# Feed-forward stage of a cross-attention block: inner Hadamard rotation in blocks of 128 on TensorE, one more butterfly level on VectorE and GpSimd, and half the down projection ahead of the transposes

## What is computed

```python
def fwht(x):            # Hadamard transform along the last axis, n a power of 2
    h = 1
    while h < n:
        x = x.reshape(-1, n // (2 * h), 2, h)
        a, b = (x[:, :, 0, :], x[:, :, 1, :])
        x = jnp.stack([a + b, a - b], axis=2).reshape(-1, n)
        h *= 2
    return (x * (1.0 / np.sqrt(n))).reshape(orig_shape)

def h_bitlinear(x, w):
    xq = act_quant(fwht(x))     # per token: scale to 127 by the largest magnitude, round
    wq = weight_quant(w)        # -1, 0 or 1 times one scale
    return jnp.einsum('bsh,oh->bso', xq, wq)
gate = h_bitlinear(hidden_states, w_gate)       # 512 -> 2048
up = h_bitlinear(hidden_states, w_up)
return h_bitlinear(jax.nn.silu(gate) * up, w_down)   # fwht over 2048, then 2048 -> 512
...
x = x + _L0_xattn_ref(_layernorm(x, axis=-1), ctx_1024, ...)
x = x + _L0_ffn_ref(_layernorm(x, axis=-1), ...)
```

## Time and profile before

| | us |
|---|---|
| median of 3 runs | 1434.11 |
| lowest, highest | 1431.78, 1435.32 |
| the profiled execution, its own time | 1431.52 |
| its span | 1429.4 |
| TensorE busy (share of the span) | 1396.0 (98%) |
| VectorE, ScalarE | 943.6, 943.4 (66% each) |
| GpSimd | 514.5 (36%) |

### The profile page before, as it was taken

How to read it: one execution, slowest core, us unless ns; L and a number is a source line. 1 busy time by engine, 2 the same in 40 slices (tenths; PEclk the granted TensorE clock), 3 DMA queues, 4 the chain that set the end, 5 groups by cost and what they waited for, 6 DMA issues and landing times. The chain is left out here.

```text
span 1429.4 us, 25937 instructions
## 1 busy us (share of the span) xinstructions
PE 1396.0 (98%) x8471; PEld 1198.2 (84%) x8471; DVE 943.6 (66%) x2401; ACT 943.4 (66%) x2068; POOL 514.5 (36%) x320
## 2 busy tenths in 40 slices
PE   8999989999999999999999999998999999999998
PEld 7999868999999999999999999997766677767775
DVE  5312047677777777777777777765466777767775
ACT  4556668888888888888888888887424333433432
POOL 0033324433322333322333322334244656455643
PEclk9999999999999999999999999999999999999999
DMA  7867722334444444344434444335533222332211
GB/s 233 223 190 203 221 71 81 106 107 111 121 133 127 113 120 117 113 133 126 118 111 122 123 118 132 92 91 153 173 95 94 60 67 60 99 71 60 66 31 44
DMA packets 171414, 165.45 MB, mean 116 GB/s; under 512 B 78274, under 2 KB 145874, under 8 KB 169490
## 3 DMA queue, kind: packets, MB, share of 16 engines
q1 hardware_dynamic: 164368, 151.21, 38.1%
q10 hardware_dynamic: 6912, 12.59, 2.6%
HBM read 123.44 MB, written 33.14 MB: 110 GB/s over the span
## 5 line engine op out<-in xcount | busy, mean ns | idle before, releaser
L714 POOL TENSOR_TENSOR rk_sp<-ms_sp,neg_half 76x10 f32<-76x10 f32 (+1 forms) x128 | 237.2, 1870 | 574.6 <-DMA ms_sp<-ms 574.6
L1051 DVE CUSTOM_DVE_ANT_0 sc<-psS,rk 100x361 f32<-100x361 f32 x256 | 136.5, 533 | 98.1 <-PE psS L777 72.7
L902 ACT ACTIVATE pr<-ex,ri 100x361 f32<-100x361 f32 x256 | 153.7, 600 | 62.0 <-DVE ri L1041 62.0
L895 ACT ACTIVATE ex<-sc,nb,rq_all 100x361 f32<-100x361 f32 x256 | 175.9, 687 | 11.9 <-DVE nb L1060 11.6
L753 PE MATMUL psK<-cT_hi,wk_hi 128*128 128x362 f32 x512 | 169.9, 332 | 1.7 <-DVE k_lo L1022 1.7
L877 ACT ACTIVATE k_hi<-psK 128x362 fp32r<-128x362 f32 x256 | 121.4, 474 | 70.5 <-PE psK L753 68.5
L753 PE MATMUL psK<-cT_lo,wk_hi 128*128 128x362 f32 x512 | 167.6, 327 | 0.0
L753 PE MATMUL psK<-cT_hi,wk_lo 128*128 128x362 f32 x512 | 167.6, 327 | 0.0
L1022 DVE TENSOR_TENSOR k_lo<-psK,k_hi 128x362 fp32r<-128x362 f32 x256 | 134.4, 525 | 6.6 <-ACT sq L884 6.6
L805 PE MATMUL psZ<-pT_hi,cK_hi 120*128 120x400 f32 (+1 forms) x384 | 133.6, 348 | 0.0
L805 PE MATMUL psZ<-pT_lo,cK_hi 120*128 120x400 f32 (+1 forms) x384 | 132.5, 345 | 0.0
(11 more groups left out here) (182 smaller groups left out, 3553.5 us busy)
## 6 DMA issues: line engine op xcount, KB each, us to landing
rk<-rk_dram SPq DMA_DIRECT2D x64, 564.1 KB
o_in<-o_dram SPq DMA_DIRECT2D x13, 1024.0 KB, 5.9
q_dram<-q_out SPq DMA_DIRECT2D x64, 200.0 KB, 4.8
q_in<-q_dram SPq DMA_DIRECT2D x64, 200.0 KB, 5.2
o_dram<-o SPq DMA_DIRECT2D x64, 200.0 KB, 5.4
stage<-in_w_ff SPq DMA_DIRECT2D x12, 1024.0 KB, 6.3
w_in<-in_w_ff ACTq DMA_DIRECT2D x48, 256.0 KB, 2.4
cT_in<-in_ctxT SPq DMA_DIRECT2D x15, 361.0 KB, 5.4
```

The lines of the kernel that those rows point to most:

```text
L714: nc.gpsimd.tensor_tensor(rk_sp[:, cols], ms_sp[:, cols], neg_half[0:HG * SKR, :].to_broadcast([HG * SKR, n]), op=ALU.pow).then_inc(g_rk, 1)
L895: nc.scalar.activation(ex[:, h % 2, :], sc[:, h % 2, :], ACT.Exp, bias=nb[:, h % 2:h % 2 + 1], scale=factor(n), accum_out=rs[:, h % 2:h % ...
L902: nc.scalar.activation(pr[:, h, :], ex[:, h % 2, :], ACT.Copy, scale=ri[:, h % 2:h % 2 + 1]).then_inc(a_pr, 1)
L1051: nc.vector.tensor_tensor_reduce(out=sc[:, h % 2, :], in0=psS[0:SQ, 0:SK], in1=rk[:, u % 2, h, :], scale=1.0, scalar=-3.0e38, op0=ALU.mult ...
```

## The change

The transform is now split at 128 and not at 256. `rotate_hidden` multiplies each of a block's four transposed chunks of 128 features by the 128x128 corner of `had`; it was two chunks against 256 columns, twice. The level of 128 against 128 becomes one more level of sums and differences: two VectorE instructions of 2x128 for each of blocks 2 and 3 in `rotate_within`, two GpSimd instructions of 4x128 for blocks 0 and 1 in `rotate_pair0`. As there is one level more, `hid` and `half_rot` change roles from there on: the transposes read `hid`, and the waits on buffers that become free are set anew. In the middle steps the first half of the down projection stands ahead of `hidden_T` of blocks 0 and 1; the second half stays where it was. Steps for tiles 0 and 12 keep their order.

```diff
             def rotate_pair0(t):
...
-                pool.wait_ge(g_pair0, t * NB + 2)
+                pool.wait_ge(g_pair0, t * 6 + 2)
                 for b, op in enumerate((ALU.add, ALU.subtract)):
                     nc.gpsimd.tensor_tensor(hid[:, b, :], half_rot[:, 0, :], half_rot[:, 1, :], op=op).then_inc(g_pair0, 1)
+                pool.wait_ge(g_pair0, t * 6 + 4)
+                src, dst = (r[:, 0:2, :].rearrange("p n (k j) -> p (n k) j", j=P).rearrange("p (m k) j -> p m k j", k=2)
+                            for r in (hid, half_rot))
+                for k, op in enumerate((ALU.add, ALU.subtract)):
+                    nc.gpsimd.tensor_tensor(dst[:, :, k, :], src[:, :, 0, :], src[:, :, 1, :], op=op).then_inc(g_pair0, 1)
...
             def rotate_hidden(t, n):
...
-                for k in range(DIM // HB):
-                    for c in range(HC):
-                        for m in (hT_hi, hT_lo):
-                            last = nc.tensor.matmul(psB[:, n, k * HB:(k + 1) * HB], m[:, n * DC + k * HC + c, :], had[:, c, :],
-                                                    start=(c == 0 and m is hT_hi), stop=(c == HC - 1 and m is hT_lo))
+                for c in range(DC):
+                    for m in (hT_hi, hT_lo):
+                        last = nc.tensor.matmul(psB[:, n, c * P:(c + 1) * P], m[:, n * DC + c, :], had[:, 0, 0:P],
+                                                start=(m is hT_hi), stop=(m is hT_lo))
...
+                if real(i) and real(i + 1) and not late:
+                    down(i, 0, front)
                 if real(i + 1):
                     hidden_T(i + 1, 0)
                     hidden_T(i + 1, 1)
                 if isinstance(i, int) and i == TILES - 1:
                     busy(psA, 27)
+                    down(i, 0, front)
                 if real(i) and not late:
-                    down(i, 0, front)
                     down(i, 1, front)
...
             def rotate_within(t, n):
...
+                dve.wait_ge(v_pair1, t * 10 + 4 * (n - 2) + 2)
+                src, dst = (r[:, n, :].rearrange("p (m k j) -> p m k j", k=2, j=P) for r in (half_rot, hid))
+                for k, op in enumerate((ALU.add, ALU.subtract)):
+                    nc.vector.tensor_tensor(dst[:, :, k, :], src[:, :, 0, :], src[:, :, 1, :], op).then_inc(v_pair1, 1)
...
             def rotate_across(t):
...
-                nc.vector.tensor_tensor(half_rot[:, 0:2, :], hid[:, 0:2, :], hid[:, 2:4, :], ALU.add).then_inc(v_r2, 1)
+                dve.wait_ge(v_pair1, t * 10 + 10)
+                dve.wait_ge(g_pair0, t * 6 + 6)
+                nc.vector.tensor_tensor(hid[:, 0:2, :], half_rot[:, 0:2, :], half_rot[:, 2:4, :], ALU.add).then_inc(v_r2, 1)
```

More of the change, by code:

```diff
@@ L1284, in rotate_pair0 @@
                 pool.wait_ge(v_h, t * NB + 2)
-                if due(t * NB):
-                    pool.wait_ge(p_hT, t * NB)
+                if due(t):
+                    pool.wait_ge(v_r2, t)
                 src, dst = (r[:, 0:2, :].rearrange("p n (k j) -> p n k j", j=HB) for r in (hid, half_rot))
@@ L1289, in rotate_pair0 @@
                     nc.gpsimd.tensor_tensor(dst[:, :, k, :], src[:, :, 0, :], src[:, :, 1, :], op=op).then_inc(g_pair0, 1)
-                pool.wait_ge(g_pair0, t * NB + 2)
+                pool.wait_ge(g_pair0, t * 6 + 2)
                 for b, op in enumerate((ALU.add, ALU.subtract)):
                     nc.gpsimd.tensor_tensor(hid[:, b, :], half_rot[:, 0, :], half_rot[:, 1, :], op=op).then_inc(g_pair0, 1)
+                pool.wait_ge(g_pair0, t * 6 + 4)
[3 more added lines that the diff above has]
+                    nc.gpsimd.tensor_tensor(dst[:, :, k, :], src[:, :, 0, :], src[:, :, 1, :], op=op).then_inc(g_pair0, 1)
             def rotate_across(t):
-                pool.wait_ge(v_pair1, t * 6 + 6)
-                pool.wait_ge(g_pair0, t * NB + NB)
-                nc.gpsimd.tensor_tensor(half_rot[:, 2:4, :], hid[:, 0:2, :], hid[:, 2:4, :], op=ALU.subtract).then_inc(g_r2, 1)
+                pool.wait_ge(v_pair1, t * 10 + 10)
+                pool.wait_ge(g_pair0, t * 6 + 6)
+                nc.gpsimd.tensor_tensor(hid[:, 2:4, :], half_rot[:, 0:2, :], half_rot[:, 2:4, :], op=ALU.subtract).then_inc(g_r2, 1)
             def result(t):
@@ L1395, in hidden_T @@
                 for c in range(DC):
-                    last = nc.tensor.transpose(psT[n % 2][:, c * P:(c + 1) * P], half_rot[:, n, c * P:(c + 1) * P], ident[:])
+                    last = nc.tensor.transpose(psT[n % 2][:, c * P:(c + 1) * P], hid[:, n, c * P:(c + 1) * P], ident[:])
                 last.then_inc(p_hT, 1)
@@ L1687, in hidden @@
                 dve.wait_ge(a_sil, t * NB + j + 1)
[L1688 to L1692, removed]
+                if j == 0 and due(t * NB):
+                    dve.wait_ge(p_hT, t * NB)
                 nc.vector.scalar_tensor_tensor(hid[:, j, :], psB[:, 2 * (j % 2) + 1, :], al[:, 1:2], sil[:, j % 2, :],
@@ L1698, in rotate_within @@
                 dve.wait_ge(v_h, t * NB + n + 1)
-                if due(t * NB):
-                    dve.wait_ge(p_hT, t * NB)
+                if n == 2 and due(t):
+                    dve.wait_ge(g_r2, t)
                 for k, op in enumerate((ALU.add, ALU.subtract)):
@@ L1703, in rotate_within @@
                                             ).then_inc(v_pair1, 1)
+                dve.wait_ge(v_pair1, t * 10 + 4 * (n - 2) + 2)
+                src, dst = (r[:, n, :].rearrange("p (m k j) -> p m k j", k=2, j=P) for r in (half_rot, hid))
+                for k, op in enumerate((ALU.add, ALU.subtract)):
+                    nc.vector.tensor_tensor(dst[:, :, k, :], src[:, :, 0, :], src[:, :, 1, :], op).then_inc(v_pair1, 1)
             def rotate_pair1(t):
[L1707 removed]
+                dve.wait_ge(v_pair1, t * 10 + 8)
                 for b, op in enumerate((ALU.add, ALU.subtract)):
[L1709 removed]
+                    nc.vector.tensor_tensor(half_rot[:, 2 + b, :], hid[:, 2, :], hid[:, 3, :], op).then_inc(v_pair1, 1)
             def rotate_across(t):
[L1713 to L1715 removed]
+                dve.wait_ge(v_pair1, t * 10 + 10)
+                dve.wait_ge(g_pair0, t * 6 + 6)
+                nc.vector.tensor_tensor(hid[:, 0:2, :], half_rot[:, 0:2, :], half_rot[:, 2:4, :], ALU.add).then_inc(v_r2, 1)
             def last_result(t):
```

## The result

The changed kernel takes 1477.08 us, the median of 5 runs (1474.34 to 1482.42), against 1435.32 for the kernel before (5 runs); the ratio is 1.030 with a 95% interval of 1.027 to 1.033. It is slower by 42 us. The profiled execution took 1482.42, its span is 1480.6, and so 51 us longer than the span of before; it was the slowest of the five.

A forecast was written before the change was run, and what follows sets the result against it. Bound by TensorE (busy 98%) and VectorE's chain, which end together. Tiles 1 to 11 add 29.7 us, tiles 0 and 12 add 7.1: 36.8 on 1431.5 gives 1468.3, stated as 1469 (range 1439 to 1481).

The forecast's parts named there:

- TensorE gains next to nothing: Rotation matmuls of 128 columns: the weight load sets 0.105 us each, saving 0.1 us a block, not 0.4.
- The chain grows by 3.75 us: VectorE's and GpSimd's sums ahead of the transposes: four new VectorE operations, held by GpSimd, end the chain 3.75 us later.
- one VectorE sum behind each GpSimd instruction: Sums ahead of the transposes: only one VectorE sum fits behind each GpSimd instruction, about 1.4 us and not 0.42.
- The half in front hides 1.7 us, 2.0 are left: Ahead of the transposes: the moved half of the down projection hides 1.7 of 3.75 us; TensorE waits about 2.0.
- the links behind decide the rest: Behind the transposes, less down projection covers VectorE: block 1's rotation starts 2.95 us later, a tile becomes 2.7 longer.
- Tiles 0 and 12, 7.1 us: First and last tile, without such cover: the whole 3.75 us less 0.2 counts, twice, 7.1 us.
- Nor does the clock fall, I think: TensorE's granted clock stays at 1.00, as in the first 60 us with 5.5 us without a matmul.
- (1): Rotation matmuls: only the columns count, 0.067 us each; 2.1 us a tile longer, 1461 us; chance 0.11.
- (3): Rotation matmuls: narrow float32r runs at the plain rate, 0.21 us; about 5.0 us a tile longer, 1499 us; chance 0.10.
- (2): VectorE's new sums aren't stretched by GpSimd: chain grows some 1.5 us, 0.55 a tile, 1441 us; chance 0.09.
- (4): TensorE alone decides, sums hidden: 1.7 us leave every tile, 1410 us; chance 0.07 with a mild form around 1425.

The follow-up runs named there:

- e8_narrow_bf16: Kernel before with rotation matmuls of 128 columns, one level of sums left out, activations' pieces and Hadamard block in bf16: 1423.20 us, ratio 0.9934.
- e4: Changed kernel without GpSimd's two new instructions a tile, VectorE's four new ones kept: 1459.22 us, ratio 1.0165.
- e9: Changed kernel with GpSimd's two new instructions replaced by two fills of about 1.38 us each that read nothing: 1460.09 us, ratio 1.0185.
- e6: Changed kernel with VectorE's two lower levels of blocks 2 and 3 done together, 4 instructions of 128x512 and not 8 of 128x256: 1477.72 us, ratio 1.032.
- e12: Changed kernel with the whole down projection ahead of the transposes of tiles 1 to 11: 1495.29 us, ratio 1.043.
- e7: Kernel before without the 13 filler matmuls ahead of tile 12's transposes: 1434.84 us against 1433.45, ratio 1.0015.
- e2: Changed kernel with the down projection back in its old place: 1499.95 us, ratio 1.045.
- e5: Changed kernel with 15 filler matmuls ahead of tile 0's transposes and 17 more ahead of tile 12's: 1472.95 us against 1432.23, ratio 1.028.
- e3: Kernel before with rotation matmuls of 128 columns and no further level of sums: 1433.34 us, ratio 0.9987.

## Why the prediction was right

It had 1469 (1439 to 1481), slower; measured were 1477. The sum of 1468.3 and the 2.6 us by which it puts the median above the profiled execution are 1470.9, not 1469. Its own addition, 36.8 us, stands against 41.8 by the medians of the two kernels.

*TensorE gains next to nothing.* I took 0.105 us a matmul between 0.067 and 0.21; measured is 0.11. e8_narrow_bf16 shows why: change the load and not the columns, and the pace halves. The Trainium skill's rule of columns divided by 1.2 (an estimate of 107 ns; "TensorE: Matmul & The Clock Gate", "LDWEIGHTS (loading the stationary operand)") holds for float32r by the 0.11; the 81 ns that the same page of the Trainium skill gives for 128 columns ("Back-to-back issue gap") was too low for float32r and too high for bf16 (0.055).

*The chain grows by 3.75 us.* Measured 3.65. The second level on block 2 was to take 1.4 us an instruction and took 1.41, on block 3 0.4 and took 0.38. That GpSimd's instructions beside the sums are the cause of the stretch, and that it is their reading, e4 and e9 show. The picture of "one VectorE sum behind each GpSimd instruction" was right for these sizes; e6 adds that GpSimd's own instructions are held in turn.

*The half in front hides 1.7 us, 2.0 are left; the links behind decide the rest.* The wait was 1.74 us. The tile grew by 2.84 us and not 2.7, and that these two are so close is in part luck. Block 1's rotation came 2.66 us later (1237.01 - 1214.75 against 1239.75 - 1220.15) and not 2.95. Up to the outer rotation, L1364 at 1240.94, the tile was 2.5 us late against 1243.85 - 1220.15 of before; q1_T, L1373 at 1245.03, was 2.85 late. The 0.35 between them are a piece that I had not looked at, VectorE's scale and GpSimd's copy in the changed kernel:

```profile
1147.77 0.22 DVE L1653 TENSOR_SCALAR al<-w,am 128x2 f32<-128x2 f32 x1
...
1243.32 0.57 DVE L1653 TENSOR_SCALAR al<-w,am 128x2 f32<-128x2 f32 x1
...
1148.00 0.62 POOL L1280 COPY x<-x 128x512 f32<-128x512 f32 x1 [0.17 <-POOL x L1277]
...
1243.25 0.62 POOL L1280 COPY x<-x 128x512 f32<-128x512 f32 x1 [0.16 <-POOL x L1277]
```

In this tile L1653 takes 0.57 us and not 0.22, and GpSimd's copy started 0.07 us ahead of it and ended with it. Before, the copy was over by then (1245.49 + 0.62 against the scale at 1246.20). I read this as a collision that the shift of the two engines against each other made. No run was made for it, but the changed kernel's trace has its own comparison, and e8_narrow_bf16's another: in the tile from 1119.19 the copy started 0.23 us behind the scale (1148.00), the scale took 0.22, and the tile took 31.63 us and not 31.96. e12 shows the larger point, that TensorE's waits can be moved about and the tile stays.

*Tiles 0 and 12, 7.1 us: this step was mis-sized.* Measured were 5.1 + 7.6 = 12.7. "Nor does the clock fall, I think" is the sentence that failed. I had looked at how much of a long stretch was idle (5.5 us of the first 60, at 1.00) where single waits of over 3 us were to be looked at. In e7 such a wait without any of the change lowers the clock, in e2 one does it in every tile, and in e5 tile 12 loses 3.4 us and not 7.6 once its wait is filled. For tile 0 that the clock makes the 1.5 us beyond the chain is read from its timeline; e5's fillers didn't keep the clock up there. With 12.7 in place of 7.1 the sum would have been 1473.9, and with the middle tiles' measured 31.2 in place of 29.7 as well, 1475.4.

*The rivals.* (1), only the columns count, and (3), plain float32's rate, fell with e3 and the 0.11 us. (2), no stretch by GpSimd, fell with e4 and e9: without the stretch the tile is 30.57 and not 31.96, which is still not 29.7, since the first new sum is held all the same. (4) would need both a shorter load and no sums; e8 has both and reaches 1423, not 1410.

## What to carry to other kernels

At 128 moving columns a matmul with fresh weights of four bytes costs its load: going from 256 to 128 freed 0.01 of 0.12 us, and a type with a shorter load freed half. Before work is split between VectorE and GpSimd, count the pairs of instructions that stand beside each other where VectorE reads both inputs from SBUF and GpSimd reads SBUF as well: they took turns here. A GpSimd instruction whose result isn't needed for a long time can set the end through them. Where waits on TensorE grow, add the low clock behind them to the price: single waits of 3.15 us and more had it each time, shorter ones some of the time. Useful work in the middle of such a wait was worth more than its length (1.7 us of down projection gave 2.2 us a tile against e2_no_move). Fillers did so in tile 12, and in tile 0 they made things worse.

## What the runs showed of the hardware that I had not expected

A single wait of 3.15 to 3.83 us on TensorE came with a granted clock of 0.50 each time that it was seen, for 3 to 14 us, and one of 1.74 us never did. That isn't a line between the two: one of 1.70 us in tile 0 was followed by 0.50 for some 7 us in e3_narrow_only and by 1.00 in the kernel before, and one of 2.42 us in e4_no_gp_level's tile 12 by 0.54 from 1431 to 1446. Two waits of 1.35 and 0.69 us were followed by it in some tiles and not in others, with the same waits. So the same timeline may or may not lose the clock, and only the runs tell. GpSimd's own sums grow when VectorE's instructions become wider: 1.4 us each with VectorE's 128x256 beside them, 1.6 with 128x512, 1.27 with neither.
